# Attention over head groups: its loop of four units written out in full, operand stacks in three slots loaded two groups ahead, values read in place

## What is computed

```python
# "nested" (it stands twice in the plan): 8 heads of width 16, projections whose input
# is narrowed by quarters of the sequence, residual added
attn = jnp.einsum('bhqd,bhkd->bhqk', q, k) * d ** -0.5
attn = jax.nn.softmax(attn, axis=-1)
attn_out = jnp.einsum('bhqk,bhkd->bhqd', attn, v)
# "wide" (once): 16 heads of width 8, scores scaled by 1/sqrt(D)
scores = jnp.einsum('bqhd,bkhd->bhqk', q, k)
out = jnp.einsum('bhqk,bkhd->bqhd', jax.nn.softmax(scores, axis=-1), v)
```

## Time and profile before

| what | value |
|---|---|
| median of 3 runs | 3769.32 us |
| the profiled execution's own time | 3765.51 us |
| its span, first to last instruction | 3763.8 us |
| instructions | 61047 |
| PE busy | 3126.6 us (83%) |
| DVE busy | 2793.6 us (74%) |
| ACT busy | 1868.8 us (50%) |
| POOL busy | 438.7 us (12%) |
| nested1 attend stage, about | 275 to 705 us |
| wide attend stage, about | 830 to 1577 us |
| nested2 attend stage, about | 1715 to 2153 us |

### The profile page before, as it was taken

One profiled execution on the slowest core, in us unless ns is written; L12 is line 12 of the kernel. 1 busy time (PEld: TensorE's weight loads), 2 busy tenths in 40 slices (PEclk: granted clock), 3 DMA queues, 4 the chain that ended last, 5 costly groups with the idle time before them and its releaser, 6 DMA issues. The chain is left out here.

```text
span 3763.8 us, 61047 instructions
## 1 busy us (share of the span) xinstructions
PE 3126.6 (83%) x19914; PEld 1782.2 (47%) x19914; DVE 2793.6 (74%) x4370; ACT 1868.8 (50%) x3233; POOL 438.7 (12%) x495
## 2 busy tenths in 40 slices
PE   6758898848888889847898979958999777759998
PEld 4533333422222223333333457656777544447776
DVE  5658877389888888547777434469999776679998
ACT  2215767517877778614767611214444444424443
POOL 0140000040000000050000001031222000032222
PEclk9857989868999999956989868859999888859999
DMA  0051212030000111041222010011111000011111
GB/s 25 15 123 25 42 29 46 5 95 16 31 30 31 33 32 40 1 95 45 46 47 46 2 24 1 0 46 46 45 45 45 4 1 0 9 52 45 45 45 53
DMA packets 74816, 131.97 MB, mean 35 GB/s; under 512 B 13872, under 2 KB 30288, under 8 KB 74576
## 3 DMA queue, kind: packets, MB, share of 16 engines
q1 hardware_dynamic: 74576, 128.75, 14.1%
HBM read 85.72 MB, written 25.43 MB: 30 GB/s over the span
## 5 line engine op out<-in xcount | busy, mean ns | idle before, releaser
L728 DVE TENSOR_REDUCE nested_a_halves<-banks 128x2 f32<-128x1024 f32 x512 | 615.9, 1222 | 132.7 <-PE banks L834 129.6
L728 DVE TENSOR_REDUCE wide_a_halves<-banks 128x2 f32<-128x1024 f32 x512 | 594.7, 1218 | 80.8 <-PE banks L834 80.5
L784 ACT ACTIVATE nested_a_p<-banks 128x512 f32<-128x512 f32 x1024 | 554.5, 597 | 201.2 <-PE banks L858 184.7
L784 ACT ACTIVATE wide_a_p<-banks 128x512 f32<-128x512 f32 x1024 | 554.1, 598 | 89.0 <-PE banks L858 66.9
L1678 ACT ACTIVATE mix_e_h<-banks,mix_b_folded 128x512 f32<-128x512 f32 x512 | 353.5, 690 | 391.8 <-PE banks L1691 383.7
L1642 DVE TENSOR_TENSOR mix_e_h_low<-mix_e_h,mix_e_h_high 128x512 fp32r<-128x512 f32 x512 | 464.0, 906 | 17.5
L834 PE MATMUL banks<-nested_k_stack,nested_q_stack 48*128 48x512 f32 x1024 | 283.0, 547 | 88.8 <-DMA nested_q_stack<-nested_q_parts 46.5
L872 PE MATMUL banks<-nested_a_p,nested_v 128*32 128x256 f32 x4096 | 345.9, 419 | 0.0
L872 PE MATMUL banks<-wide_a_p,wide_v 128*32 128x256 f32 x4096 | 333.1, 404 | 11.1 <-issue 11.1
L858 PE MATMUL banks<-nested_q_stack,nested_k_stack 50*128 50x512 f32 x1024 | 262.1, 444 | 10.1 <-ACT nested_a_p L784 9.6
L834 PE MATMUL banks<-wide_k_stack,wide_q_stack 48*128 48x512 bf16 x1024 | 211.7, 410 | 59.1 <-issue 18.5
(11 more groups left out here) (367 smaller groups left out, 4575.3 us busy)
## 6 DMA issues: line engine op xcount, KB each, us to landing
mix_e_gate<-mix_gates_t SPq DMA_DIRECT2D x128, 256.0 KB, 3.2
nested_q_stack<-nested_q_parts SPq DMA_DIRECT2D x96, 128.0 KB
nested_q_parts<-nested_p_q_cut SPq DMA_DIRECT2D x16, 512.0 KB
nested_k_parts<-nested_p_k_cut SPq DMA_DIRECT2D x16, 512.0 KB
nested_k_stack<-nested_k_parts SPq DMA_DIRECT2D x32, 256.0 KB
nested_v<-nested_values SPq DMA_DIRECT2D x16, 512.0 KB, 10.1
wide_v<-wide_values SPq DMA_DIRECT2D x16, 512.0 KB, 3.0
wide_q_stack<-wide_q_parts SPq DMA_DIRECT2D x192, 32.0 KB
```

What stands on the lines that cost most here:

```text
L728: dve.tensor_reduce(halves[:, half, i, 2 * a:2 * a + 2], bank[:, at:at + 2, :], AX, ALU.max).then_inc(maxed, 1)
L784: act.activation(p[:, kt % 4, j, :], bank[:, ST + n % RING, :], ACT.Exp, scale=scale).then_inc(probs, 1)
```

## The change

It does four things in the three attention layers.

1. The stacks have three slots (`SLOTS = 3`), and group n uses slot n % 3. POOL's fill of `k_stack` grows with it, from 4096 to 6144 elements for each partition.
2. The copy of a group's values is gone. `mix_values` reads `hd.values[:, u // 2, ...]`. The waits on it are gone too, and SP's wait on `v_copied` before the first loads.
3. The loop is gone: every engine's program is written out for all 16 or 32 units, with constants for semaphores and addresses.
4. SP's program is ordered anew. Group 2 is loaded at the start of the stage. For even u from 2 on, SP waits until all of unit u-1's shifted scores are done (`shifted`, 32 for each unit), loads group u/2 + 2, and behind that issues the shift rows of unit u. That is 5 loads of this kind in each nested layer and 13 in wide.

```diff
-                src = self.q_parts[bass.ds(n, 1), :, h, a].rearrange("o s e t -> e (o s) t")
+                src = self.q_parts[n, :, h, a].rearrange("s e t -> e s t")
...
-        sp.dma_start(self.v[:, k], self.values[:, bass.ds(n, 1)].rearrange("p o i c -> p (o i) c")).then_inc(
-            self.v_in[k], 16)
...
                 sp.wait_ge(parts_out, 32 * hd.parts)
-                sp.wait_ge(v_copied, 2 * hd.groups)
-                for k in range(2):
-                    hd.load(sp, k, k)
+                for n in range(2):
+                    hd.load(sp, n)
...
+    def slot(u):
+
+        return u // 2 % SLOTS
+
+    def loaded(u):
+
+        return (u // 2 // SLOTS + 1) * 16 * LOADS
...
-                shift_load(0, 0)
                 sp.wait_ge(hd.parts_out, 32 * hd.parts * B)
-
-                def turn(it, first, last):
-                    for ui in range(4):
-                        u, k = it * 4 + ui, ui // 2
-                        if ui % 2 == 0 and not (first and k == 0) and not (last and k == 1):
-                            sp.wait_ge(mixed, u * TILES)
-                            hd.load(sp, it * 2 + k + 1, (k + 1) % 2)
-                        if not (last and ui == 3):
-                            shift_load(u + 1, ui + 1)
-
-                turns(sp, hd.total // 2, turn)
+                hd.load(sp, 2)
+                for u in range(UNITS):
+                    if u >= 2 and u % 2 == 0 and u // 2 + 2 < hd.total:
+
+                        sp.wait_ge(shifted, u * ITEMS)
+                        hd.load(sp, u // 2 + 2)
+                    shift_load(u)
...
-                def scores(u, ui, m, k, qc):
+                def scores(u, m):
 
                     a, i, half = m // 8, m // 2 % 4, m % 2
-                    at, q_at = place(ui, m), qc * T2 + i * P
+                    at, q_at = place(u, m), u % 2 * T2 + i * P
+                    if u % 2 == 0 and m == 0:
+                        pe.wait_ge(qk_in[slot(u)], loaded(u))
...
+                def shifted_scores(u, n):
+
+                    kt, j = n // 4, n % 4
+                    if n == 0:
+                        pe.wait_ge(shift_in, (u + 1) * SHIFT_LOADS)
...
-                        last = pe.matmul(bank[32 * j:32 * j + 32, MIX, cols], v[:, k, kt, 32 * j:32 * j + 32],
-                                         p[:, kt % 4, j, cols], start=(kt == 0 and c == 0),
-                                         stop=(kt == TILES - 1 and c == 1))
+                        last = pe.matmul(bank[32 * j:32 * j + 32, MIX, cols],
+                                         hd.values[:, u // 2, kt, 32 * j:32 * j + 32], p[:, kt % 4, j, cols],
+                                         start=(kt == 0 and c == 0), stop=(kt == TILES - 1 and c == 1))
...
-                turns(pe, hd.total // 2, turn)
+                for u in range(UNITS):
+                    for kt in range(TILES):
```

More of the change, by code:

```diff
@@ L344 @@
     GROUP = 4
+    SLOTS = 3
     def __init__(self, core, ctx, name, heads, kind):
@@ L387, in rows_of, with load @@
         return slice(base, base + self.rows + extra), j // self.per_tile
-    def load(self, sp, n, k):
+    def load(self, sp, n):
+        k = n % self.SLOTS
         for h in range(self.per_tile):
@@ L696, in _, with shift_load @@
             def _(sp):
-                def shift_load(u, ui):
-                    k, qc = ui % 4 // 2, ui % 2
+                def shift_load(u):
+                    qc = u % 2
                     sp.wait_ge(shift_copied, u + 1)
@@ L863, in wait_for_bank @@
                     last = n - RING if n >= RING else max(range(n, ITEMS, RING)) - ITEMS
                     wait_past(pe, probs, u * ITEMS + (last + 1))
-                def mix_values(s, kt, k, c):
+                    rows, slab = hd.rows_of(j, 2)
+                    pe.matmul(bank[:, ST + n % RING, :], k_stack[rows, slot(u), slab, kt * P:(kt + 1) * P],
+                              q_stack[rows, slot(u), slab, u % 2 * T2:(u % 2 + 1) * T2],
+                              start=True, stop=True).then_inc(shifted, 1)
@@ L935, in _ @@
-                turns(pe, hd.total // 2, turn)
-                for h in range(2):
-                    mix_values(UNITS * TILES - 1, TILES - 1, 1, h)
-                pe.wait_ge(mix_copied, UNITS)
-                pe.wait_ge(written, UNITS - 2)
-                turn_mix(UNITS - 1, special_place(4))
+                    scores(1, m)
+                for n in range(RING):
+                    shifted_scores(0, n)
+                for u in range(UNITS):
+                    for kt in range(TILES):
+                        for h in range(2):
+                            m = 2 * kt + h
+                            if kt < 4 and u + 1 < UNITS:
+                                scores(u + 1, m + PAIRS // 2)
+                            if kt >= 4 and u + 2 < UNITS:
+                                scores(u + 2, m - PAIRS // 2)
+                            for n in range(4 * kt + 2 * h + RING, 4 * kt + 2 * h + 2 + RING):
+                                if n < ITEMS:
+                                    shifted_scores(u, n)
+                                elif u + 1 < UNITS:
+                                    shifted_scores(u + 1, n - ITEMS)
+                            if kt:
+                                mix_values(u, kt - 1, h)
+                            elif h == 0 and u:
+                                for c in range(2):
+                                    mix_values(u - 1, TILES - 1, c)
+                            if kt == 4 and h == 1:
+                                pe.wait_ge(maxed, min((u + 2) * PAIRS + 1, UNITS * PAIRS))
+                                if u + 1 < UNITS:
+                                    turn_shifts(u + 1)
+                                if u:
+                                    turn_mix(u - 1)
@@ L943, in turns @@
+                for c in range(2):
+                    mix_values(UNITS - 1, TILES - 1, c)
+                wait_past(pe, written, UNITS - 2)
+                turn_mix(UNITS - 1)
 def turns(engine, count, turn):
```

177 lines of the change are left out of this document (57 added, 120 removed).

## The result

The changed kernel takes **3952.01 us** (median of 4 runs, 3942.14 to 3962.48). The kernel before, run beside it, takes 3768.86 us (4 runs, 3755.0 to 3776.37). The ratio is **1.0491 [1.0443, 1.0539]**: 4.9% slower. Forecast were 3940 us and a range of 3862 to 4015. The profiled execution of the changed kernel took 3942.5 us, 177.0 more than the 3765.5 of before.

The account below looks back on a forecast made before the run. The prediction took DVE as nearly full in clean units, with PE, on which it waits, setting the rest. From 3765.5 us, +331 stalls, -152 gains and -9 project stages gave 3935.5, so about 3940 us; range 3862 to 4015.

Parts of the forecast that it names:

- the last paragraph of the prediction: Signs expected in the profile after: 23 PE waits for shift rows, some 270 us, no stack waits, no loop idle.
- The stalls, +331 forecast: Attend stages: PE waits for shift rows behind each load, 10 times in nested (166 us), 13 in wide (165).
- The clock was taken as 2.8: Behind each stall in the attend stages: low PE clock costs 2.8 us, bounds 2.3 and 6.
- The low end for nested: Nested stall if shift rows overtake the load's data: 8.3 us.
- The high end, 14.7: Nested stall if rows land like the values' copy, last DMA of the old load: 14.7 us.
- the clock stays low: Rival, attend stages: 6 us of low clock a stall and both high ends, 4036 us; chance 0.06 for beyond 4015.
- The gains, -152 forecast: Attend stages: every unit becomes clean, without stack waits, loop turns and low clock; 46, 46 and 60 us saved.
- The project stages, -9 forecast: Project stages: dropped values' copies shorten DVE's store waits, POOL's larger fill costs some back; together -9 us.
- I take -6 for each nested stage: Nested project stages: DVE waits less for stores without the two 0.5 MB copies, 6 us saved each.
- -2.5 in wide: Wide's project stage: DVE's store wait shrinks by 2.5 us, as SP's issues fill more of the time.
- The +1.8 for the fill: Project stages: POOL's fill grows from 3.54 to 5.3 us, charged as 1.8 us three times.
- Loading early wins: Rival, attend stages: the stall is hidden or short, only -152 and -9 remain, 3608 us; chance 0.05.

Follow-up runs that it names:

- e1: Changed kernel, but SP issues a unit's shift rows ahead of that unit's load, not behind it; 3604.96 us, ratio 0.9582 to the kernel before.
- e4: Changed kernel, but shift rows of the 23 units behind a load are issued on ACT's DMA queue; 3812.71 us, ratio 1.0109 to the kernel before.
- e8: Changed kernel with the shift rows issued in the middle of the load instead of behind it; 3854.08 us, ratio 1.0242 to the kernel before.
- e7: Changed kernel with the values' copy (0.5 MB, four slots) put back at each load's end, ahead of the shift rows; 3992.94 us, ratio 1.0595.
- e2: Changed kernel with two slots and SP's order of the kernel before, still written out, values read in place; 3703.57 us, ratio 0.9823.
- e3: e2 with the values' copy put back: the kernel before with only the loop written out; 3730.98 us, ratio 0.9861 to the kernel before.
- e6: e1 (shift rows ahead of the load) with the values' copy put back; 3628.72 us, ratio 0.9604 to the kernel before.
- e9: e1 with early loads spread out: load 0 behind store 2, load 1 behind store 3, load 2 behind unit 0's rows; 3593.78 us, ratio 0.9539.

## Why the prediction was right

**The mechanism.** All that the last paragraph of the prediction asked for is there: 23 waits at `shifted_scores`, 10 and 13, each behind the last load issue; no wait of `scores` for a stack; no idle "issue" stretch of a loop; odd units clean but for one. e1 shows that the order on SP's queue is the cause. e4 and e8 show what the price is made of: in wide the issues ahead of the rows (6.0 of 10.0 us) and the late moment of the rows' own issue (4.0), in nested both and the data.

**The stalls, +331 forecast.** The waits were taken as 13.8 and 9.9 us and measured 13.5 and 10.0. The clock was taken as 2.8 and measured 2.9 and 2.3. Ten times 16.4 and thirteen times 12.2 are 323 us. The low end for nested, 8.3 us, was refused for rows that come at the same place in the queue. On SP's queue that was right, 13.5 us; on ACT's (e4) PE was released after 7.5 us. The high end, 14.7, was priced with the values' copy ahead of the rows, and e7, which has it, waits 14.9. The rule that the prediction takes from the Trainium skill, page "DMA: Bandwidth & Descriptors", section "Queues, rings and completion order", that descriptors are consumed in ring order on each DMA engine, agrees with the trace in that the low end is out; the nested stalls do not stand at their high end, but 1.2 us below it.

**The stretches of low clock outside stalls, no term of the sum.** The difference of the changed kernel and e1 in the attend stages is 83.1 + 161.4 + 95.5 = 340 us, 17 more than the stalls. It lies in three units of the profiled execution, 8.1 + 2.6 + 8.1 us, less some 2 us in the first units. The first stands beside a stall in nested2, where the unit behind the stalled one is 30.1 us instead of 22.0:

```profile
2065.40:2087.40 22.00, 21.51 (x202) 9.13 (x204) 20.41 (x21) 18.35 (x34) 0.00 (x0) 1.00 0.01 2
2087.40:2125.90 38.50, 24.64 (x202) 9.91 (x204) 20.41 (x21) 18.48 (x35) 0.00 (x0) 0.78 0.28 42
2125.90:2156.00 30.10, 30.07 (x202) 11.79 (x204) 20.71 (x21) 18.44 (x35) 0.00 (x0) 0.66 0.01 1
```

PE is busy for all of the third stretch, mostly at 1.2 GHz. It is the rival "the clock stays low", at a higher price than the 6 us given for it (2.9 in the stalled unit and 8.1 behind it), but one time in 23. The same happened once in e4 (30.0 us) and twice in e7 (29.4 and 30.0), and never in e8. The other two are the last units of wide (18.8 instead of 16.2) and of nested2 (25.6 instead of 17.5). Of these two the second isn't the change's: in the profiled execution of before the same unit was 27.0 us.

**The gains, -152 forecast.** From before to e1 the attend stages lose 45.1 + 60.3 + 50.8 = 156 us, against 46, 60 and 46. The forecast was made for the pairs of units alone, and these lose 46.7 + 59.7 + 45.9 = 152.3 us, as forecast. The rest is nested2's last unit, 9.4 us, and wide's, 1.3, less 7.1 us by which the three first units are longer in e1; these vary as much from kernel to kernel. The split by e2 is new, again by pairs: the written-out loop and the values in place give wide 51 of its 60 us, and each nested layer 6.5; the third slot and the earlier loads give 8 in wide and 40 in each nested layer.

**The project stages, -9 forecast, -6.0 measured.** The term "I take -6 for each nested stage" was too large, and "-2.5 in wide" too small: DVE's waits for the stores fell by 2.9 us in each nested stage (77.4 to 71.6 for two) and by 3.8 in wide (13.3 to 9.5). The term was priced as bytes by the rate of the stacks' load; e7 shows the same thing, with 1.4 us where the bytes give 3.5. The longest of these waits, 24.37 in the earlier trace rows, is now:

```profile
187.07 13.33 DVE L539 TENSOR_SCALAR nested_p_h<-x_resident,nested_p_ln_moments,nested_p_both 128x128 f32<-128x128 f32 x8 [7.56 <-POOL x_resident L505]
194.50 5.25 POOL L520 MEMSET nested_k_stack<- 128x6144 f32 x1
...
247.38 0.69 DVE L551 CAST nested_p_q_cut<-nested_p_q_t 128x1024 fp32r<-128x1024 f32 x1 [21.35 <-DMA nested_k_parts<-nested_p_k_cut]
```

The +1.8 for the fill is confirmed by the same rows: DVE's eight instructions take 13.33 us instead of 11.62, and the fill 5.25 instead of 3.54. Whether it reaches the end is less sure: start and gaps together are 600.4 us in e2, which fills two slots, 3.6 to 5.6 less than in the four kernels of the table that fill three; but with the copy put back, e3 with two slots (617.1) is not shorter than e6 and e7 with three (615.6 and 618.8).

**The sum.** Against the execution before, 323 + 17 - 156 - 6 = 178 us, where 177.0 were measured. Forecast was 170, and the median lies 9.5 us above the profiled execution where 3.8 was taken from before. These two make the 12 us between 3940 and 3952. Part of the closeness is luck: the low clock in single units, 17 us here, was no term of the sum, and half of it is made up by stalls that were forecast 8 us too dear.

**The rivals.** "Loading early wins", 3608 us, is what e1 measures (3605), so its price was right and only its condition fails: a stall costs 16.4 or 12.2 us, above the 7.0 at which it decides. With rows on ACT's queue a stalled unit is 10.5 us too long in nested and 6.5 in wide, 8.2 on average and so near that point, and e4 comes out 1.1% slower. The rule of the Trainium skill, page "DMA: Bandwidth & Descriptors", section "Rules for kernel authors", to issue a DMA early and wait on it late, holds on this evidence for the stacks (in e1 `scores` waits for none); for the rows the changed kernel breaks it, and e1 restores it.

## What to carry to other kernels

SP issued its queue strictly in order here, waits included, so a bulk load that is moved earlier must not be moved ahead of a small transfer that is due sooner: here the same early load made the kernel 4.2% faster behind that transfer and 4.9% slower ahead of it. Price such a wait from what stands ahead of it, the issues first (18 of them were 6.2 us) and the bytes second, and add some 2 to 3 us of low clock to each wait, long or short: it was 2.3 to 3.0 behind waits of 4.0 to 13.5 us in the changed kernel, e4 and e8. When a load goes to its new place, write down for each DMA behind it who waits for it and when; if the order can't be changed, another engine's queue takes the issues away (here 6 us of each stall) but not the late moment at which the transfer may start, and, as far as nested shows, not all of the data.

## What was not expected of the hardware

- Half a megabyte copied over 128 partitions cost the rows behind it 1.3 to 1.4 us, although the stacks of the same load, few partitions each, keep the DMA engines 91% busy at 149 GB/s, at which the copy would take 3.5. The same copy at the end of a load (e3) came with 9 us more of waits for stacks in wide.
- PE at work without a wait can have its clock lowered: the last unit of a nested stage took 17.5 us at clock 1.00 in e1, 22.8 at 0.70 in e9, and 25.6 to 27.0 in one nested stage each of before, the changed kernel, e2, e4, e6 and e7 and in both of e8, with the same matmuls.
- A turn of a loop in wide cost some 7 to 9 us of the two units around it, for 5.9 us of idle time. In nested it was 3 to 4.
- An issue on SP's queue was not of fixed length: one `L400` DMA took 0.42 us in the attend stage and 2.13 in e9's project stage, where stores and loads were under way. Why isn't shown.
